# State space stage: y summed over the states in SBUF instead of in PSUM

## The reference

```
xz = x @ W_in.T;  u, z = split(xz)
uc = silu(conv3(u) + conv_b)
dtp, Bm, Cm = split(uc @ W_xproj.T)          # 64, 16 and 16 columns
dt = softplus(dtp @ W_dt.T + b_dt);  A = -exp(A_log)
for t: h = exp(dt_t * A) * h + B_t * u_t     # h: 16 states x 512 channels
       y_t = sum over n of C_t[n] * h[n]
y = (y + D * uc) * silu(z);  out = y @ W_out.T
```

## Time and profile before

| | |
|---|---|
| median of 3 runs | 4415.19 us |
| the profiled execution | 4434.16 us, span 4432.1 us |
| busy: PE, DVE, ACT, POOL | 3956.1, 2631.5, 1531.7, 1320.7 us |
| granted clock of TensorE, mean of the span | 0.949 |
| start of the first and the last scan | 81.6 us, 1164.1 us |

### The profile page before, as it was taken

The page is one execution under the profiler, slowest core; times in us unless marked ns, Lnnn a source line. Parts: engine busy times, 40 slices in busy tenths (PEclk is TensorE's granted clock), DMA queues, the critical chain, the costliest instruction groups (busy, mean ns, idle before and its releaser), DMA issues. The chain is left out here.

```text
span 4432.1 us, 66912 instructions
## 1 busy us (share of the span) xinstructions
PE 3956.1 (89%) x23304; PEld 2705.7 (61%) x23304; DVE 2631.5 (59%) x4638; ACT 1531.7 (35%) x2950; POOL 1320.7 (30%) x1340
## 2 busy tenths in 40 slices
PE   5788878888699999999998989999989899999799
PEld 3566666666544688888885655555545455555444
DVE  3878788778566455555554446666633366666333
ACT  4655555555200122222221124444411144444111
POOL 2656566566300000000001223333310133333111
PEclk8999889888899999999998989999999899999899
DMA  1000000000200100000002210000021100010210
GB/s 36 1 10 10 1 10 10 10 1 5 77 29 29 36 10 10 11 9 9 11 9 95 70 52 29 28 28 28 25 79 43 47 24 28 28 28 26 67 57 33
DMA packets 154012, 127.77 MB, mean 29 GB/s; under 512 B 24968, under 2 KB 151544, under 8 KB 153496
## 3 DMA queue, kind: packets, MB, share of 16 engines
q1 hardware_dynamic: 153880, 126.04, 9.1%
HBM read 88.23 MB, written 37.77 MB: 28 GB/s over the span
## 5 line engine op out<-in xcount | busy, mean ns | idle before, releaser
L346 POOL TENSOR_SCALAR ssm_ub<-ssm_uT,ssm_bT 128x512 f32<-128x512 f32 x512 | 356.7, 716 | 387.7 <-PE ssm_pu L861 326.7
L861 PE MATMUL ssm_pu<-ident,ssm_ub 128*128 128x128 f32 x2048 | 347.5, 297 | 117.7 <-DVE ssm_state L652 102.1
L2051 POOL TENSOR_TENSOR win_rotated<-win_straight,win_turned 128x512 f32<-128x512 f32 x128 | 162.4, 1269 | 749.2 <-DVE win_turned L2158 749.2
L861 PEld LDWEIGHTS ssm_pu<-ident,ssm_ub 128*128 128x128 f32 x2048 | 267.8, 155 | 175.4 <-DVE ssm_state L652 89.2
L652 DVE TENSOR_TENSOR_SCAN ssm_state<-ssm_da,ssm_carry,ssm_pu 128x512 f32<-128x512 f32 x256 | 320.3, 1271 | 84.9 <-PE ssm_pu L861 84.3
L2265 PE MATMUL win_pa<-win_w_wqkv,win_hT 128*128 128x512 f32 x768 | 364.5, 611 | 1.3 <-ACT win_hT L2074 1.1
L652 DVE TENSOR_TENSOR_SCAN ssm_state<-ssm_da,ssm_pu 128x512 f32<-128x512 f32 x256 | 306.0, 1211 | 85.3 <-PE ssm_pu L861 84.6
L2094 ACT ACTIVATE win_probs<-win_sc,win_nbias,win_rn 128x256 f32<-128x256 f32 x512 | 284.3, 566 | 208.7 <-DVE win_nbias L2182 208.6
L871 PE MATMUL ssm_py<-ident,ssm_seen 128*128 128x128 f32 x2048 | 329.3, 303 | 28.5 <-DVE ssm_seen L662 16.1
L871 PEld LDWEIGHTS ssm_py<-ident,ssm_seen 128*128 128x128 f32 x2048 | 275.7, 158 | 125.4 <-issue 86.2
L1871 PE MATMUL glu_up<-glu_hT,glu_w_w 128*128 128x512 f32 x640 | 293.0, 615 | 26.7 <-DVE glu_act L1819 23.1
(11 more groups left out here) (253 smaller groups left out, 7604.6 us busy)
## 6 DMA issues: line engine op xcount, KB each, us to landing
win_raw<-in_tables SPq DMA_DIRECT2D x64, 128.0 KB, 2.1
a<-win_y SPq DMA_DIRECT2D x64, 128.0 KB, 1.7
glu_xs<-a SPq DMA_DIRECT2D x32, 256.0 KB, 3.2
glu_x<-a SPq DMA_DIRECT2D x16, 512.0 KB, 4.9
ssm_x<-in_L_attn_x SPq DMA_DIRECT2D x8, 512.0 KB, 3.7
x<-ssm_out SPq DMA_DIRECT2D x16, 256.0 KB, 2.2
moe_x<-x SPq DMA_DIRECT2D x8, 512.0 KB, 3.8
x<-moe_y SPq DMA_DIRECT2D x8, 512.0 KB, 2.9
```

What stands on the lines that cost most here:

```text
L346: nc.gpsimd.tensor_scalar(ub[:, i % 2, t, :], uT[:, k % 2, t, :], bT[:, k % 2, t, n:n + 1], 1.0, ALU.mult, ALU.mult).then_inc(ub_ready.sem, 1)
L861: last = nc.tensor.transpose(pu[c % 2][:, t * P:(t + 1) * P], ub[:, i % 2, t, c * P:(c + 1) * P], ident)
```

## The change

The states are turned back to tokens on the partitions one by one, so that C is a scalar per partition, and y grows in SBUF (`acc`). `transpose_state(i, t)` turns token tile t of a state into a bank of pt: even tiles into pt0, odd ones into pt1. DVE's `add_even` multiplies an even tile by C and adds it to acc in one instruction; for an odd tile ACT's `weigh` multiplies it into `weighted` and POOL's `add_odd` adds it. `begin_sum` (POOL) starts acc with D * uc, for which D is broadcast once. The matrix pick, the split of C in three bf16 parts, the spread, py, pc, the skip's transposes and seen go. The PSUM that comes free gives four banks pu (inject(i + 1, c) waits for scan (i, c) alone) and two banks pf. The sum of a block is transposed before it is gated (steps 18 and 19), z is computed with channels on the partitions (steps 6 and 7), and the gated tiles need no copy.

```diff
-        seen = s.sb("seen", [P, 2, CT, BLK])
-        c_rows = s.sb("c_rows", [P, 2, BLK])
+        weighted = s.sb("weighted", [P, 2, HID])
+        acc = s.sb("acc", [P, 2, TB, HID])
         carry = s.sb("carry", [P, NS, CT])
...
-        py = [s.ps(f"py{t}", [P, HID]) for t in range(TB)]
-        pu = [s.ps(f"pu{k}", [P, BLK]) for k in range(2)]
-        pc, pf = s.ps("pc", [P, BLK]), s.ps("pf", [P, BLK])
+        pu = [s.ps(f"pu{c}", [P, BLK]) for c in range(CT)]
+        pt = [s.ps(f"pt{j}", [P, HID]) for j in range(2)]
+        pf = [s.ps(f"pf{j}", [P, BLK]) for j in range(2)]
...
-            def weigh_high(i):
-                pool.wait_ge(c_copied.sem, c_copied.at(i))
-                pool.wait_ge(state_ready.sem, state_ready.at(i))
-                pool.wait_ge(added2.sem, added2.at(i - 2))
-                nc.gpsimd.tensor_tensor(seen[:, i % 2, high, :], state[:, i % 2, high, :],
-                                        c_rows[:, i % 2, :].unsqueeze(1).to_broadcast([P, 2, BLK]),
-                                        ALU.mult).then_inc(seen_high.sem, 1)
+            def begin_sum(k, t):
+                pool.wait_ge(uT_ready.sem, uT_ready.at(k, t + 1))
+                pool.wait_ge(turned_made.sem, turned_made.at(k - 2))
+                nc.gpsimd.tensor_tensor(acc[:, k % 2, t, :], uT[:, k % 2, t, :], skip[:, :], ALU.mult).then_inc(begun.sem, 1)
+
+            def add_odd(i, j):
+                k, t = i // NS, 2 * j + 1
+                if i % NS == 0:
+                    pool.wait_ge(begun.sem, begun.at(k))
+                pool.wait_ge(weighed.sem, weighed.at(i, j + 1))
+                pool.wait_ge(sums_odd.sem, sums_odd.at(i - 1, j + 1))
+                nc.gpsimd.tensor_tensor(acc[:, k % 2, t, :], acc[:, k % 2, t, :], weighted[:, j, :], ALU.add)\
+                  .then_inc(sums_odd.sem, 1)
 
             for i in range(FIRST, END):
                 if 0 <= i + 1 < N * NS:
                     scale_u(i + 1)
                 if 0 <= i - 1 < N * NS:
-                    weigh_high(i - 1)
+                    add_odd(i - 1, 0)
+                    add_odd(i - 1, 1)
                 for k in range(N):
-                    if i == k * NS - 18:
+                    if i == k * NS - 1:
+                        begin_sum(k, 0)
+                        begin_sum(k, 1)
+                    elif i == k * NS:
+                        begin_sum(k, 2)
+                        begin_sum(k, 3)
+                    elif i == k * NS - 18:
...
-            def copy_c(i):
-                act.wait_ge(seen_high.sem, seen_high.at(i - 2))
-                act.wait_ge(c_made.sem, c_made.at(i))
-                nc.scalar.activation(c_rows[:, i % 2, :], pc[:, :], ACT.Copy).then_inc(c_copied.sem, 1)
+            def weigh(i, j):
+                k, t = i // NS, 2 * j + 1
+                act.wait_ge(state_turned.sem, state_turned.at(i, 2 * j + 2))
+                act.wait_ge(sums_odd.sem, sums_odd.at(i - 1, j + 1))
+                nc.scalar.activation(weighted[:, j, :], pt[1][:, :], ACT.Copy,
+                                     scale=bcT[:, k % 2, t, NS + i % NS:NS + i % NS + 1]).then_inc(weighed.sem, 1)
...
-                if 0 <= i < N * NS:
-                    copy_c(i)
+                if (i + 1) % NS and 0 <= i + 1 < N * NS:
+                    step_decay(i + 1, 0)
+                if 0 <= i - 1 < N * NS:
+                    weigh(i - 1, 0)
                 second_product(i - 1)
-                if (i + 1) % NS == 0:
-                    first_product(i)
-                if 0 <= i + 1 < N * NS:
+                if (i + 1) % NS and 0 <= i + 1 < N * NS:
+                    step_decay(i + 1, 1)
+                if 0 <= i - 1 < N * NS:
+                    weigh(i - 1, 1)
+                first_product(i)
+                if (i + 1) % NS == 0 and 0 <= i + 1 < N * NS:
                     step_decay(i + 1, 0)
-                if (i + 1) % NS:
-                    first_product(i)
-                if 0 <= i + 1 < N * NS:
...
-            def gate(k, t):
-                if t == 0:
+            def gate(k, c):
+                if c == 0:
                     dve.wait_ge(z_ready.sem, z_ready.at(k))
-                    dve.wait_ge(added2.sem, added2.at(k * NS + NS - 1))
-                nc.vector.tensor_tensor(gated[:, t, :], py[t][:, :], z[:, t, :], ALU.mult).then_inc(gated_ready.sem, 1)
+                dve.wait_ge(turned_made.sem, turned_made.at(k, c + 1))
+                nc.vector.tensor_tensor(gatedT[:, c, :], pf[c % 2][:, :], z[:, c, :], ALU.mult).then_inc(gated_ready.sem, 1)
...
-                elif c == 2:
-                    dve.wait_ge(seen_high.sem, seen_high.at(i - 2))
+                    dve.wait_ge(state_turned.sem, state_turned.at(i - 2))
                 dve.wait_ge(bu_made.sem, bu_made.at(i, c + 1))
-                nc.vector.tensor_tensor_scan(state[:, i % 2, c, :], da[:, i % 2, c, :], pu[c % 2][:, :],
+                nc.vector.tensor_tensor_scan(state[:, i % 2, c, :], da[:, i % 2, c, :], pu[c][:, :],
                                              carry[:, n, c:c + 1] if k % 2 else 0.0,
...
-            def weigh_low(i, c):
-                if c == 0:
-                    dve.wait_ge(c_copied.sem, c_copied.at(i))
-                dve.wait_ge(state_ready.sem, state_ready.at(i, c + 1))
-                freed = added1 if c else added0
-                dve.wait_ge(freed.sem, freed.at(i - 2))
-                nc.vector.tensor_tensor(seen[:, i % 2, c, :], state[:, i % 2, c, :], pc[:, :], ALU.mult).then_inc(seen_low.sem, 1)
+            def add_even(i, j):
+                k, t = i // NS, 2 * j
+                if i % NS == 0:
+                    dve.wait_ge(begun.sem, begun.at(k, t + 1))
+                dve.wait_ge(sums_even.sem, sums_even.at(i - 1, j + 1))
+                dve.wait_ge(state_turned.sem, state_turned.at(i, t + 1))
+                nc.vector.scalar_tensor_tensor(acc[:, k % 2, t, :], pt[0][:, :],
+                                               bcT[:, k % 2, t, NS + i % NS:NS + i % NS + 1], acc[:, k % 2, t, :],
+                                               ALU.mult, ALU.add).then_inc(sums_even.sem, 1)
 
             for i in range(FIRST, END):
-                scanning = 0 <= i < N * NS
+                scanning, behind = 0 <= i < N * NS, 0 <= i - 1 < N * NS
                 if scanning:
                     scan(i, 0)
-                after_first_scan(i)
-                if scanning:
                     scan(i, 1)
                 after_second_scan(i)
+                if behind:
+                    add_even(i - 1, 0)
                 if scanning:
-                    weigh_low(i, 0)
                     scan(i, 2)
                     scan(i, 3)
-                    weigh_low(i, 1)
+                if behind:
+                    add_even(i - 1, 1)
                 rest_of_step(i)
...
             def inject(i, c):
                 if c == 0:
                     pe.wait_ge(ub_ready.sem, ub_ready.at(i))
-                if c < 2:
-                    pe.wait_ge(state_ready.sem, state_ready.at(i - 1, c + 3))
+                pe.wait_ge(state_ready.sem, state_ready.at(i - 1, c + 1))
+                for t in range(TB):
+                    last = nc.tensor.transpose(pu[c][:, t * P:(t + 1) * P], ub[:, i % 2, t, c * P:(c + 1) * P], ident)
+                last.then_inc(bu_made.sem, 1)
+
+            def transpose_state(i, t):
+                if t == 0:
+                    pe.wait_ge(state_ready.sem, state_ready.at(i))
+                j = t // 2 + 1
+                if t % 2:
+                    pe.wait_ge(weighed.sem, weighed.at(i, j - 1) if j == 2 else weighed.at(i - 1))
                 else:
-                    pe.wait_ge(state_ready.sem, state_ready.at(i, c - 1))
-                for t in range(TB):
-                    last = nc.tensor.transpose(pu[c % 2][:, t * P:(t + 1) * P], ub[:, i % 2, t, c * P:(c + 1) * P], ident)
-                last.then_inc(bu_made.sem, 1)
-
...
+                    pe.wait_ge(sums_even.sem, sums_even.at(i, j - 1) if j == 2 else sums_even.at(i - 1))
+                for c in range(CT):
+                    last = nc.tensor.transpose(pt[t % 2][:, c * P:(c + 1) * P], state[:, i % 2, c, t * P:(t + 1) * P], ident)
+                last.then_inc(state_turned.sem, 1)
 
...
-                n = i % NS
-                scanning, ahead, behind = 0 <= i < N * NS, 0 <= i + 1 < N * NS, 0 <= i - 1 < N * NS
-                if scanning:
-                    inject(i, 2)
+                    pe.wait_ge(weights, 16 * 8)
+                ahead, behind = 0 <= i + 1 < N * NS, 0 <= i - 1 < N * NS
+                if behind:
+                    transpose_state(i - 1, 0)
+                    transpose_state(i - 1, 1)
+                turn_ends = i % NS == NS - 1
                 first_product(i, 0)
-                if behind and n != 1:
-                    gather(i - 1, 1)
-                add_skip(i)
-                if scanning:
-                    inject(i, 3)
```

(46 more changed lines are left out.)

338 lines of the change are left out of this document (142 added, 196 removed).

## The result

The changed kernel takes 4447.31 us, median of 5 runs (4434.98 to 4457.66), against 4415.19 (also 5 runs, 4410.66 to 4424.8) before: ratio 1.0068, 95% interval 1.0044 to 1.0092. It is slower by 0.7%. The forecast was 4465.

A forecast was written before the change was run, and what follows sets the result against it. A new POOL-PE-ACT ring would bound the steps, plus lower-clock cost: middle blocks +34, block 0 +12.7, block 7 +16.5, start and end -13, total +50 us, giving 4465; range 4375 to 4550.

The forecast's parts named there:

- The ring: Each scan step: POOL's scaling of u, PE's transposes, ACT's weighing and POOL's second sum wait in a circle, 6.7 us.
- The block's end: Step 14 to 15: scaling waits for the last turned u, 13.5 us; step 15 to 16: POOL's sums and scaling, 7.8.
- The convolutions: Steps 5 and 6: VectorE has 10.4 us of work in each, the ring gives 7.6; about 0.8 us left over.
- The clock: PE falls to its lower clock after waits in steps without front products, costing 12 us a middle block.
- rival B: Clock low in nearly all steps without front products: 22 us a block in place of 12, 4545 us; chance 0.20.
- Block 0: First block of scans, no old block behind it: 141.4 us, +12.7 on 128.7.
- block 7: Last block of scans, no front work ahead: 127.6 us with 12 for the clock, +16.5 on 111.1.
- The start: Start of the stage: six waits for the only front bank go, and the path by C's parts: -9 us.
- The end: End of the stage: four copies and part of the gating leave the chain, -4 us.
- C: Whole stage faster: ring as summed, clock does not fall, each block keeps the removed stalls, 4369 us; chance 0.18.
- D: Scan steps: the ring does not close, POOL runs ahead and DVE alone bounds, 4230 us; chance 0.05.
- E: ACT's queue holds the weighing in three more steps of a block by 2.3 us each, 4521 us; chance 0.07.

The follow-up runs named there:

- two cuts: Changed kernel with POOL scaling u one step earlier: 4299.1 us; changed kernel with PE transposing state tiles 2 and 3 ahead of inject 0 and 1: 4309.68 us.
- the run with extra work: Changed kernel with eight extra PE transposes of the identity ahead of inject 0 in eight steps of a block: 4420.33 us, ratio 0.9991.
- the cut kernels: Changed kernel with POOL scaling u earlier: 4299.1 us; the same with the block end reordered and an edge copy given to ACT: 4253.85 us.

## Why the prediction was right, and where it was off

- **The ring** (6.7 us a step) was right: 6.76. Each member is there at its price: two groups of 1.04, ACT 0.69, POOL 1.27 and 2.69. Shown by two cuts, and by the added POOL instruction in a step at the upper clock. Over the stage the fused sum and the weighing were priced within 2% (means of 740 and 686 ns).
- **The block's end** (13.5 from step 14 to 15, 7.8 to the next) was right: 13.4 and 7.6. (The terms as listed add up to 13.32 and not 13.35.)
- **The convolutions** (0.8 us left over) were mis-sized. I let VectorE's 2 x 10.4 us run into its 3.3 us of lead and the ring's 2 x 7.6. The two steps took 21.2 us of the changed kernel, with VectorE busy for 20.2:

```profile
389.00:410.20 21.20, 17.87 (x101) 11.74 (x100) 20.17 (x22) 13.92 (x23) 15.19 (x15) 1.00 0.00 1
```

  VectorE bounds there. Not all of the 5 us over the 16.0 of the sum is lost, as the scan step behind them takes 5.8 to 6.0 and not 7.6. From scaling to scaling the three steps concerned take 8.65, 9.21 and 10.82 us in block 2, where the ring, the front product and the residual make 7.6, 7.6 and 10.3: 3.3 left over, 2.5 more than in the sum. The three dt steps take 7.97 each at the upper clock, for 7.56: 1.2 more.
- **The clock** (12 us a block) was too dear. It was also to be seen as 0.80 to 0.86 in the middle blocks, and it was 0.91, above the 0.89 of before. The changed kernel's windows for four steps running, each with a wait of 3.0 to 3.05 us, and for a block's end:

```profile
1153.70:1180.70 27.00, 14.86 (x130) 13.83 (x128) 24.56 (x26) 13.78 (x16) 20.72 (x24) 1.00 0.01 1
```

```profile
478.10:489.40 11.30, 3.75 (x26) 3.28 (x27) 7.76 (x7) 8.02 (x13) 8.17 (x11) 0.79 0.00 0
```

  In the first the clock stays at its upper level, where the earlier trace rows had shown a fall behind 3.33 us; in the second, with waits of 3.49 and 4.06, it falls. What a fall costs is seen where one step stands at both levels. From the scaling for step 9 to the next, in block 4 and in block 2:

```profile
709.17:716.80 7.63, 4.88 (x33) 4.43 (x34) 4.13 (x5) 3.33 (x5) 5.17 (x7) 1.00 0.01 2
419.34:428.48 9.14, 6.40 (x32) 5.83 (x33) 4.34 (x5) 3.32 (x5) 5.17 (x7) 0.81 0.00 0
```

  Here 1.5 us; 1.3 in step 14 (7.98 and 9.26), 0.8 in step 3 (7.21 and 8.04). The mean of each step of blocks 1 to 6 less its time at the upper level, added up over the nine steps that fell in some block, is 7 to 8 us a block (an estimate, as two of the nine never stood at the upper level throughout a middle block). The 7.5 by the run with extra work agrees. So the measured 144.2 are some 7.7 for the clock and 136.5 without it, where 12 and 133.0 stood, with 1.5 for POOL and VectorE slowing each other: 3.5 too few in the order and 5.8 too many in the other two, so that 2.3 too many were left.
- **The page** "TensorE: Matmul & The Clock Gate" of the Trainium skill (HAM oscillation) tells of a kernel whose clock falls in the wait behind every burst. That every such step would be low (rival B), as I took from it, is not borne out by the first of these windows.
- **Block 0** +6.9 for +12.7 and **block 7** +8.8 for +16.5: both held 12 us of clock, more than it cost in the middle blocks; what it cost in these two was not worked out. **The start** gained more than said: the first scan is at 65.9 us for 81.6, -15.7 where -9 stood (-14.1 against the second trace of before); that it was the six waits for the only front bank was not tested. **The end**: from the last scan's end to the last output's, 20.7 us for 25.9, -5 where -4 stood.
- Sum of the stage: 6 x 3.4 + 6.9 + 8.8 - 15.7 - 5 = +15, against +50 forecast; the medians say +32. So the sign and the cause stood, and 4465 was 18 us high. That it was no more is in part luck: by the traces the stage grew by a third of what was forecast, and from the 4426 that the kernel before took later, +50 would have been 4476.
- **The rivals.** C (faster, if the clock costs under 5.8 a block) did not have its condition, as the clock cost 7 to 8. D (no ring) is what the cut kernels show: 4299, and 4254 with the rest removed, not 4230. E (ACT's queue, 2.3 us more in three steps) was not tested by itself, but the trace leaves no room for it: Exp and Ln stand in the step of 13.4 us (13.5 in the sum) and the normalising in one of 7.6 (7.8 in the sum).
- **The signs.** POOL's wait for ACT, PE's wait for POOL, the steps of 6.76 us and the wait for pt in place of that for pu came as said. The granted clock did not, and neither did POOL idle for over 7 us at a block's end: between its second sum (to 478.81) and the scaling at 485.44 lie 6.6 us, with small instructions in them.
